# A gated feed-forward kernel on one core: the first two tiles by interleaved column blocks, and the start-up order of all engines

## What is computed

```
scale = cond @ norm_w.T + 1.0
ms = jnp.mean(x * x, axis=-1, keepdims=True)
h = x * (scale[:, None, :] * jax.lax.rsqrt(ms + EPS))
u = h @ up_w.T
val, gate = jnp.split(u, 2, axis=-1)
h = val * jax.nn.gelu(gate, approximate=False)
hq = act_quant(h)          # to 8-bit steps, one scale per token
wq = weight_quant(down_w)  # to -1, 0, 1 times the mean of |down_w|
y = hq @ wq.T
return y + x
```

## Time and profile before

| | |
|---|---|
| three runs | 429.4 us median (429.03 to 429.54) |
| the profiled execution | 429.27 us, span of its instructions 427.5 us |
| TensorE matmul, busy | 421.1 us, 99% of the span |
| TensorE weight load | 337.6 us, 79% |
| VectorE | 280.4 us, 66% |
| ScalarE | 186.4 us, 44% |
| GpSimd | 179.9 us, 42% |

### The profile page before, as it was taken

The page is one execution under the profiler, slowest core; times in us unless marked ns, Lnnn a source line. Parts: engine busy times, 40 slices in busy tenths (PEclk is TensorE's granted clock), DMA queues, the critical chain, the costliest instruction groups (busy, mean ns, idle before and its releaser), DMA issues.

```text
span 427.5 us, 7667 instructions
## 1 busy us (share of the span) xinstructions
PE 421.1 (99%) x2081; PEld 337.6 (79%) x2081; DVE 280.4 (66%) x539; ACT 186.4 (44%) x334; POOL 179.9 (42%) x323
## 2 busy tenths in 40 slices
PE   7999999999999999999999999999999999999997
PEld 5688888888887888887888888888878888878786
DVE  4987567556577566576565675565675665765676
ACT  5753444443444444444434444434444434444441
POOL 1564435435345344354344354353453353553520
PEclk9999999999999999999999999999999999999999
DMA  8434443334444334434244433343443344342324
GB/s 281 147 80 115 100 118 103 75 97 123 98 105 115 71 100 106 115 98 107 74 114 98 120 100 77 94 123 98 108 113 73 98 111 109 98 108 75 87 51 124
DMA packets 82024, 45.01 MB, mean 105 GB/s; under 512 B 68256, under 2 KB 68704, under 8 KB 81888
## 3 DMA queue, kind: packets, MB, share of 16 engines
q1 hardware_dynamic: 81584, 44.33, 39.8%
q10 hardware_dynamic: 432, 0.59, 0.4%
HBM read 20.00 MB, written 8.39 MB: 66 GB/s over the span
## 4 chain that ended last, share of the span: by engine, by line
PE 94%; DMA 1%; DVE 1%; SPq 1%; POOL 1%; issue 1%; ACT 0%; DVEq 0%; POOLq 0%
PE p_gate L678 41%; PE p_val L678 41%; PE p_y L698 12%; DMA up_raw<-up_w_t 1%; SPq L219 1%; DVE y_sb L500 0%; PE p_val L650 0%; POOL a_hi L311 0%; POOL scaled L308 0%; PE p_gate L650 0%; DVE q_rounded L526 0%; DVE h L547 0%; PE p_gate L657 0%; POOL a_lo L315 0%; DVE last_max L509 0%
## 5 line engine op out<-in xcount | busy, mean ns | idle before, releaser
L547 DVE SCALAR_TENSOR_TENSOR h<-p_val,rstd,gelu 128x512 f32<-128x512 f32 x128 | 95.3, 746 | 129.9 <-PE p_val L678 129.5
L389 ACT ACTIVATE gelu<-p_gate,rstd 128x512 f32<-128x512 f32 x128 | 87.5, 684 | 149.1 <-PE p_gate L678 139.4
L304 POOL TENSOR_TENSOR mean_sq_eps<-mean_sq,rms_eps 128x1 f32<-128x1 f32 x64 | 12.2, 190 | 224.3 <-PE p_val L678 210.3
L361 ACT ACTIVATE q<-q_rounded 128x1024 bf16<-128x1024 f32 x63 | 66.7, 1058 | 78.2 <-DVE q_rounded L582 78.2
L678 PE MATMUL p_gate<-up_hi,a_lo 128*128 128x512 f32 x248 | 80.6, 406 | 0.6 <-POOL a_lo L315 0.6
L678 PE MATMUL p_val<-up_hi,a_hi 128*128 128x512 f32 x248 | 78.2, 396 | 0.0
L678 PE MATMUL p_val<-up_hi,a_lo 128*128 128x512 f32 x248 | 78.1, 396 | 0.0
L678 PE MATMUL p_val<-up_lo,a_hi 128*128 128x512 f32 x248 | 78.1, 396 | 0.0
L678 PE MATMUL p_gate<-up_lo,a_hi 128*128 128x512 f32 x248 | 78.1, 395 | 0.0
L678 PE MATMUL p_gate<-up_hi,a_hi 128*128 128x512 f32 x248 | 78.1, 395 | 0.0
L568 DVE TENSOR_REDUCE h_max<-h 128x1 f32<-128x1024 f32 x63 | 76.6, 1216 | 1.2
(11 more groups left out here) (74 smaller groups left out, 247.1 us busy)
## 6 DMA issues: line engine op xcount, KB each, us to landing
xt_in<-x_t SPq DMA_DIRECT2D x32, 256.0 KB, 2.8
x_all<-x SPq DMA_DIRECT2D x32, 256.0 KB, 2.9
out<-y_sb SPq DMA_DIRECT2D x31, 256.0 KB, 2.0
up_raw<-up_w_t SPq DMA_DIRECT2D x6, 256.0 KB, 5.4
down_raw<-down_w_t SPq DMA_DIRECT2D x1, 1024.0 KB, 8.0
q_t<-q SPq DMA_TRANSPOSE x63, 3.1
up_raw<-up_w_t ACTq DMA_DIRECT2D x2, 256.0 KB, 3.1
out<-y_sb SPq DMA_DIRECT2D x1, 128.0 KB, 2.0
```

Of the source, the lines that this page charges most:

```text
L304: pool.tensor_tensor(mean_sq_eps[:, j:j + 1], mean_sq[:, j:j + 1], rms_eps[:, :], ALU.add).then_inc(pool_step, 1)
L361: act.activation(q[j % 2][:, :], q_rounded[j % 2][:, :], ACT.Copy, bias=-ROUND).then_inc(q_ready, 1)
L389: act.activation(gelu[c][:, :], p_gate[c][:, :], ACT.Gelu, scale=rstd[:, j:j + 1]).then_inc(gelu_done, 1)
L547: nc.vector.scalar_tensor_tensor(h[s][:, c * W:(c + 1) * W], p_val[c][:, :], rstd[:, j:j + 1], gelu[c][:, :], op0=ALU.mult, op1=ALU.mult). ...
```

## The change

What it does, engine by engine:

- **Transfers.** `cond_norm` is the only load on ScalarE's queue; all of `up_raw` goes through SyncE's, with `xt_in` of tiles 0 and 1 second, and `down_raw` behind all weights and the second `xt_in`. The next unit's first loads no longer wait behind the first DMA transpose.
- **TensorE.** 13 dummy matmuls ahead of the scale and 2 behind it, for 7 and 4. Tiles 0 and 1 are formed together for column half 0 (`first_blocks`), tile 0 in `p_gate0` and `p_val0`, tile 1 in `p_gate1` and `p_val1`; then half 1 of tile 0 and half 1 of tile 1 (`second_block`) in the same banks.
- **VectorE and ScalarE.** Their operations of tiles 0 and 1 are written out in a new order, mixed with the weight pieces. `a_hi` of both tiles is made early, half by half. The last ternary pass is gone from VectorE: its second pass clips both ways, and ScalarE makes `down_t` in tile 2, after that tile's second gelu. Both passes of VectorE stand in tile 2.
- **GpSimd.** Only `mean_sq_eps` and `rstd` for tiles 0 and 1. `a_hi` and `a_lo` have four buffers each, not two, and in the loop GpSimd may start a tile when value banks up to three tiles before are done, not two.

The core of the diff:

```diff
-        a_hi = [sb(f"a_hi{i}", [P, KD, P], fp32r) for i in range(2)]
-        a_lo = [sb(f"a_lo{i}", [P, KD, P], fp32r) for i in range(2)]
+        a_hi = [sb(f"a_hi{i}", [P, KD, P], fp32r) for i in range(UNIT)]
+        a_lo = [sb(f"a_lo{i}", [P, KD, P], fp32r) for i in range(UNIT)]
...
+            load_up(0, 0)
+            load_xt(0, 0)
+            load_up(0, 1)
+            load_up(1, 0)
+            load_up(1, 1)
+            load_x(0, 0)
+            for c in (2, 3):
                 for k in range(KD):
-                    sp.dma_start(up_raw[:, c, k, :], up_w_t[c // 2, c % 2, :, k, :]).then_inc(up_in[c * KD + k], 16)
-            sp.dma_start(cond_norm_sb[:, :], cond_norm).then_inc(cond_norm_in, 16)
-            load_xt(0, 0)
-            load_up(1)
-            load_up(2)
-            load_x(0, 0)
-            load_up(3)
+                    load_up(c, k)
+            load_xt(0, 1)
             sp.dma_start(down_raw[:, :, :], down_w_t).then_inc(down_in, 16)
-            load_xt(0, 1)
             load_x(0, 1)
+            sp.wait_ge(first_a_ready, TPB)
+            load_xt(1, 0)
+            sp.wait_ge(squares_done, TPB)
+            load_x(1, 0)
...
+            mean(0, 0)
+            root(0, 4)
+            mean(1, 1)
+            root(1, 5)
+            for j in range(TPB, UNIT):
+                if j % TPB == 0:
+                    pool.wait_ge(xt_landed[j // TPB], 16)
+                product(0, j)
+                low_part(j, BEFORE + PER_TILE * (j - 2) + 2)
+                mean(j, j)
+                root(j, BEFORE + PER_TILE * (j - 2) + 3)
+            with pool.Fori(1, UNITS) as u:
                 for j in range(UNIT):
-                    tile(u, j, first)
-            units(pool, unit)
+                    t = UNIT * u + j
+                    step = BEFORE + PER_TILE * (t - 2)
+                    if j % TPB == 0:
+                        pool.wait_ge(xt_landed[j // TPB], 16 * (u + 1))
+                    pool.wait_ge(val_done, NP * (t - 2))
+                    mean(t, j)
+                    product(u, j)
+                    low_part(j, step + 3)
+                    root(j, step + 3)
...
+            act.dma_start(cond_norm_sb[:, :], cond_norm).then_inc(cond_norm_in, 16)
+            act.preload_act_table(ACT.Gelu)
+            high_part(0, 0)
+            act.wait_ge(xt_landed[0], 16)
             for k in range(KD):
-                act.dma_start(up_raw[:, 0, k, :], up_w_t[0, 0, :, k, :]).then_inc(up_in[k], 16)
-            act.preload_act_table(ACT.Gelu)
-            for c in range(NP * 2):
-                for k in range(KD):
-                    act.wait_ge(up_in[c * KD + k], 16)
-                    act.activation(up_hi[:, c, k, :], up_raw[:, c, k, :], ACT.Copy).then_inc(up_hi_ready, 1)
-                if c == 2:
-                    square(0, 0, True)
-            act.wait_ge(xt_landed[0], 16)
-            act.wait_ge(scale_ready, 1)
+                act.wait_ge(scale_ready, k + 1)
+                act.activation(a_hi[1][:, k, :], xt_in[0][:, k, 1, :], ACT.Copy,
+                               scale=scale_t[:, k, 0:1]).then_inc(second_a_hi_ready, 1)
+            high_part(0, 1)
             for k in range(KD):
-                last = act.activation(a_hi[1][:, k, :], xt_in[0][:, k, 1, :], ACT.Copy, scale=scale_t[:, k, 0:1])
-            last.then_inc(second_a_hi_ready, 1)
+                high_part(1, k)
+            square(0, 0, True)
+            square(0, 1, True)
+            high_part(2, 0)
+            early_gelu(0, 0)
+            high_part(2, 1)
+            high_part(3, 0)
+            high_part(3, 1)
+            early_gelu(1, 0)
+            early_gelu(0, 1)
+            act.wait_ge(down_in, 16)
+            act.activation(down_tmp[:, :, :], down_raw[:, :, :], ACT.Abs, accum_out=abs_sum[:, :]).then_inc(abs_ready, 1)
+            square(0, 2)
+            early_gelu(1, 1)
+            integers(0, 0, True)
+            square(0, 3)
...
+                for j in range(TPB if first else 0, UNIT):
...
+                    if first and j == TPB:
+                        act.wait_ge(ternary_step, 4)
+                        act.activation(down_t[:, :, :], down_tmp[:, :, :], ACT.Copy, bias=-ROUND).then_inc(down_ready, 1)
...
-            nc.vector.memset(warm[:, :], 0.0).then_inc(warm_ready, 1)
+            nc.vector.memset(warm[:, :], 1.0).then_inc(warm_ready, 1)
...
+                dve.wait_ge(scale_done, k + 1)
+                nc.vector.tensor_scalar(scale_t[:, k, :], scale_bank[k][:, 0:B], 1.0, None,
+                                        ALU.add).then_inc(scale_ready, 1)
+                dve.wait_ge(xt_landed[0], 16)
+                dve.wait_ge(scale_ready, k + 1)
                 nc.vector.tensor_scalar(a_hi[0][:, k, :], xt_in[0][:, k, 0, :], scale_t[:, k, 0:1], None,
                                         ALU.mult).then_inc(a_hi_ready, 1)
...
+            def early_h(t, c):
+                n = early(t, c)
+                dve.wait_ge(rstd_ready, t + 1)
+                dve.wait_ge(val_done, n + 1)
+                dve.wait_ge(gelu_done, n + 1)
+                nc.vector.scalar_tensor_tensor(h[t][:, c * W:(c + 1) * W], p_val[t][:, :], rstd[:, t:t + 1],
+                                               gelu[t][:, :], op0=ALU.mult, op1=ALU.mult).then_inc(h_done, 1)
...
-                    nc.vector.tensor_scalar(down_tmp[:, :, :], down_tmp[:, :, :], ROUND, 1.0,
-                                            ALU.subtract, ALU.min).then_inc(ternary_step, 1)
-                if stage == 2:
-                    dve.wait_ge(ternary_step, 4)
-                    nc.vector.tensor_scalar(down_t[:, :, :], down_tmp[:, :, :], -1.0, None,
-                                            ALU.max).then_inc(down_ready, 1)
+                    nc.vector.tensor_scalar(down_tmp[:, :, :], down_tmp[:, :, :], ROUND + 1.0, ROUND - 1.0,
+                                            ALU.min, ALU.max).then_inc(ternary_step, 1)
...
+            dve.wait_ge(a_hi_ready, KD)
+            x_low_part(0)
+            low_part(0, 0)
+            dve.wait_ge(second_a_hi_ready, KD)
+            x_low_part(1)
+            low_part(0, 1)
+            for k in range(KD):
+                low_part(1, k)
+            low_part(2, 0)
+            early_h(0, 0)
+            low_part(2, 1)
+            low_part(3, 0)
+            low_part(3, 1)
+            early_h(1, 0)
+            early_h(0, 1)
+            quantised(0, 0, 0)
+            early_h(1, 1)
+            quantised(0, 1, 1)
...
+                        if first and j == TPB:
+                            ternary(c)
+                        if first and j == TPB and c == 0:
+                            for done in range(TPB):
+                                rescale(0, done)
...
-            keep_busy(7)
+            keep_busy(13)
...
+                nc.tensor.matmul(scale_bank[k][:, 0:B], cond_norm_sb[:, B + k * P:B + (k + 1) * P],
+                                 cond_norm_sb[:, 0:B], start=True, stop=True).then_inc(scale_done, 1)
+            keep_busy(2)
+            def first_blocks():
+                for which, banks, done in ((0, p_gate, gate_done), (1, p_val, val_done)):
                     for k in range(KD):
-                        if j == 0:
+                        piece = which * KD + k + 1
+                        hi, lo = up_hi[:, which, k, :], up_lo[:, which, k, :]
+                        pe.wait_ge(up_hi_ready, piece)
+                        pe.wait_ge(a_hi_ready, k + 1)
+                        nc.tensor.matmul(banks[0][:, :], a_hi[0][:, k, :], hi, start=(k == 0), stop=False)
+                        pe.wait_ge(second_a_hi_ready, k + 1)
+                        nc.tensor.matmul(banks[1][:, :], a_hi[1][:, k, :], hi, start=(k == 0), stop=False)
+                        pe.wait_ge(first_a_ready, 1)
+                        nc.tensor.matmul(banks[0][:, :], a_lo[0][:, k, :], hi, start=False, stop=False)
+                        if piece > 1:
+                            nc.tensor.matmul(banks[1][:, :], a_lo[1][:, k, :], hi, start=False, stop=False)
+                        pe.wait_ge(up_lo_ready, piece)
+                        last = [nc.tensor.matmul(banks[t][:, :], a_hi[t][:, k, :], lo, start=False, stop=(k == KD - 1))
+                                for t in range(TPB)]
+                        if piece == 1:
+                            pe.wait_ge(first_a_ready, TPB)
+                            nc.tensor.matmul(banks[1][:, :], a_lo[1][:, k, :], hi, start=False, stop=False)
+                    for t in range(TPB):
+                        last[t].then_inc(done, 1)
...
+            def second_block(t):
+                n = early(t, 1)
+                for which, bank, done, read in ((0, p_gate[t], gate_done, gelu_done), (1, p_val[t], val_done, h_done)):
+                    col = 2 + which
+                    pe.wait_ge(read, n - 1)
+                    for k in range(KD):
+                        if t == 0:
```

(24 more changed lines are left out.)

187 lines of the change are left out of this document (69 added, 118 removed).

## The result

| | median of the device time | executions |
|---|---|---|
| before | 429.41 us (429.03 to 429.79) | 12 |
| changed | 430.48 us (429.31 to 431.53) | 12 |

The ratio is 1.0023, 95% interval 1.0016 to 1.0030: slower by 1.07 us, and outside the range 428.0 to 430.0. The eleven other executions of the changed kernel lie at 430.09 to 431.53; the one that was profiled first is the shortest of the twelve, 429.31. It is read first all the same, because it is the forecast almost line by line.

The account below looks back on a forecast made before the run. TensorE's pace bounds the loop, so only tile 4's start counts: 30.5 us by the chain of late operands, plus 0.6 for two terms, is 31.1, 0.25 earlier than 31.35, giving 429.0 us; range 428.0 to 430.0.

Parts of the forecast that it names:

- the bound: Whole kernel: TensorE at its pace limits the loop, so what is won or lost at tile 4 stays to the end.
- the new wait: Ahead of tile 4, first of the loop: TensorE waits for GpSimd's `a_lo`, 1.2 us of the 2.05 won; chance 0.58.
- V: Start-up on TensorE: start of the matmul that completes tile 0's first value bank, forecast at 11.4 us.
- the 0.4 for the shared ports: Start-up: VectorE and GpSimd get in each other's way; bounds nothing and three times 0.45 us, 0.4 taken.
- TensorE's own lead: Start-up to tile 4: TensorE alone would reach tile 4 at 29.3 us, 2.05 us won.
- the scale passes: Start-up on TensorE: four passes, 1.06 us, beginning when the dummies end at 3.84, with `cond_norm` taken as landed.
- rival C: First loads: `cond_norm` lands no earlier, 4.24 for 3.84 moves all by 0.4, time 429.4 us; chance 0.13.
- the start's second term: Start-up: `xt_in` may land after 4.8, the clock may rise after 7.45; bounds 0 and 0.7 us, 0.2 taken.
- Rival D: First up matmuls: gaps from 5.2 to 7.45 keep TensorE at 1.2 GHz, 0.19 us more per matmul, slower; chance 0.12.

Follow-up runs that it names:

- the engines apart: The change with GpSimd's products for tile 2 waiting for the last `up_lo`, those for tile 3 for tile 0's rounding: median 430.22 us, profiled execution 430.52.
- the first profile: Profile of the changed kernel's first measurement, its fastest execution: 429.31 us, where the median of twelve is 430.48.
- the third profile: Profile of the unedited changed kernel, measured a third time: 430.51 us, median 430.58, ratio 1.0027 to the kernel before.
- squares first: The change with the `squares` of tile 4 ahead of `down_t` on ScalarE: median 428.85 us, ratio 0.9980 to the kernel before; profiled execution 429.01.

## Why the prediction was wrong

**Right: the bound.** Time less tile 4 is 397.8 to 398.0 in thirteen of the fourteen profiles; tile 4 was the right place to take the sum. (The exception is `cond_norm` on SyncE's queue, 431.26 with tile 4 at 32.76: 398.5. Its last matmuls stand as far behind tile 4 as in the change, 424.92 - 32.76 and 423.49 - 31.33, both 392.16, so its 0.5 arose behind them.)

**Right: the new wait.** "The wait moves from tile 2 to tile 4" is what happened, with the order and sizes given: `down_t` 1.91, `squares` to mean 0.58, mean to tile 4 2.26 (2.2 forecast). From V the forecast had VectorE's first `h` at 0.44 and tile 4 at 19.1, that is 18.66 between the two; with the 0.4 for the shared ports 19.06. Measured 19.05 to 19.07, and 18.64 with the engines apart. Its size is partly luck: 0.4 was a choice between 0 and 1.35. What lies under it differs from execution to execution, too: 0.53 at the remainders and 0.08 at the first rounding in the first profile, 0.42 to 0.44 at the rounding alone in the other two.

**Wrong, but covered by that wait: TensorE's own lead.** Forecast was 2.05 us at tile 4; without the wait tile 4 of the first profile would have begun at 31.33 - 1.19 = 30.14, a lead of 1.2. The late start took 0.4, and two pairs of tile 0's second block 0.7, where the forecast had VectorE's remainders ahead. So the exchange of `squares` and `down_t` had 1.2 us to win back, not 2.

The rule that the Trainium skill states for the ports' term (SBUF — State Buffer, "Who interferes with whom") is borne out: in the first profile an `a_lo` and a remainder began within 0.01 us of each other, the `a_lo` took 1.28 for 0.74 and the next remainder 1.22 for 0.68, as if they had taken turns. By it the prediction allowed up to 0.7 for such a meeting; 0.54 was measured.

**Wrong by 0.4: the scale passes.** "I take `cond_norm` as landed" at 3.84. They began at 4.23, which is rival C's bound, 4.24, and C's condition held: it landed 3.4 us after its issue for 3.5 before. But the landing is the smaller part. With it out of the way (`cond_norm` first on SyncE's queue) the passes began at 4.08: 0.24 of the 0.39 are the dummies', of which 0.13 is that they began at 1.20, as their operand's memset takes 0.27 us for 0.17, and 0.15 is left for the landing. For the landing, the load was compared with the other queue's load instead of asking what the two did to each other: alone it takes 2.3. The Trainium skill's sentence on queues (DMA: Bandwidth & Descriptors, "Issuing engines are not separate DMA queues") had warned rightly for this load. With the 0.4, V is 11.8 and tile 4 at 31.3, which is the profiled execution.

**Wrong by 1.0 to 1.3 more, of which 0.2 had been allowed: the start's second term.** "The clock may rise after 7.45", with bounds 0 and 0.7 and 0.2 taken. This is the step that failed. In the late profiles it rises at 8.7 to 10.5, and in one it rose early and fell back. That makes the scale passes slower, the sixth matmul 0.6 to 0.75 later (0.07 and 0.22 of it are again `cond_norm`'s landing, at 4.30 and 4.45), and one to five behind it up to 0.19 each: first `h` at 13.22 and 13.52 in the change's own two, not 12.28, and tile 4 at 32.29 and 32.58, not 31.1. Rival D had the mechanism at a chance of 0.12, and its 430.3, for a rise after 10.4, is near the 430.48 measured, but it was priced from a single row, the rise before at 8.83. Two things were missed. That moment differs from execution to execution, so one profile gives no bound; and the slow passes of the scale and the slow first matmuls had to be in the price: in the third profile they are half of it, 0.60 at the sixth matmul against 0.64 behind it.

Why the kernel before doesn't pay in this way was argued from its trace, not tested: it too was slow up to 8.83, but its second column half then waited for ScalarE's last weight piece, landed near 10.9, and tile 2 for ScalarE and GpSimd. Those waits would cover a late clock. The change took them off the path, and what had been covered is now paid 1:1. The change's sum in the typical case: tile 4 later by 32.58 - 31.35 = 1.23; the medians differ by 1.07. The kernel before isn't free of long executions either: five of 35 in the first set took 430.9 to 431.2, and no trace has one.

What stays open is what lets the clock rise at 4.5 in one execution and at 10 in the next. Neither the dummies' number nor their data settled it: with seven or one ahead of the scale it came late in both profiles, and none of the eleven executions is below 430.5; with thirteen it came at 4.4 to 5.0 in four of ten profiles (and fell back in one of these); with fifteen it came after 10. The stretch of five up matmuls with gaps, to which D laid it, doesn't decide alone: the change's first profile has the same stretch as that of squares first, and only in the latter did the clock fall.

## What to carry to other kernels

A start-up path without slack inherits whatever varies between executions; before removing a wait, ask what it was covering, and take more than one profile of the start. A gain at one point is worth only what the next late operand leaves of it: the move of `down_t` onto ScalarE, ahead of the next unit's `squares`, cost 1.2 to 1.6 us, in the first profile the whole lead, and exchanging two instructions brought them back. With that exchange the change is faster than the kernel before, 428.85, ratio 0.9980 (0.9968 to 0.9991); with dummies over the gaps as well 428.63, ratio 0.9973 (0.9958 to 0.9988). And two kernels whose profiles caught different executions can't be compared by one profile each: the remainders' 2.42 or 1.89 hung on the clock, not on the edit.
